# Rows of 64 floats instead of 48 and 50 in the gathered and scattered tables of a four-layer graph network

## The chip, the cores and the metric

The kernel runs on one core of one Trainium2 chip. The metric is the device time of one execution in microseconds (us). Three runs of the kernel before took 16726.7, 16704.65 and 16701.4 us, a median of 16704.65 us.

## The reference, cut to what matters

There are 12500 nodes with 48 features and 400000 edges, sorted by destination. Four layers follow each other, each adding to `x` what it sums over the edges, with a layer norm after each:

```python
x = _layernorm(x + _L0_gnn_ref(x, edge_index, edge_attr_32, ...))      # MLP of (x[dst], x[src], edge), summed by dst
x = _layernorm(x + _L1_gnn_ref(x, src, dst, W, b))                     # x[src] * ci[src], summed by dst
x = _layernorm(x + _L2_gnn_ref(x, edge_index, W, b))                   # norm * x[dst], summed by src
x = _layernorm(x + _L3_gnn_ref(x, edge_index, edge_attr_40, ...))      # gate * x[dst] * cutoff, summed by src
```

The first two layers sum by destination, in which the edges are sorted. The last two sum by source, in which they are not.

## The kernel before, in words

The edges are cut into 125 groups of 25 tiles of 128 edges, and a group into 5 chunks of 5 tiles. A pass over all groups belongs to each layer (pass 0 to pass 3), and behind each pass stands an epilogue (e0 to e3) that works on the nodes in 10 runs of at most 10 blocks of 128 nodes. Each engine runs its own loop over the groups; semaphores alone order them, and between stages all engines meet at a barrier.

Pass 0 and pass 1 gather the source node's row for each edge with indirect DMAs that GpSimd (POOL) issues, one for each tile of 128 edges (lines 489 and 1027). The table of pass 0, `btab`, has rows of 160 floats (640 bytes). The table of pass 1, `y1`, has rows of 48 floats (192 bytes); e0 writes it. TensorE sums a chunk's rows by destination with one-hot matmuls (line 1208), and then the chunk's buffer is free for the next group.

Pass 1 also works out a place for each edge, ordered by source (`uidx`), stores the gates of layer 3 for later, and fills the DRAM tensor `order` with zeros, one store of `zero` on the ScalarE queue in each group (line 1004). `order` has a row for each edge and for padding. A row was OW = 50 floats (200 bytes): 48 features, one more for layer 3's weight, and the low 7 bits of the source (column MW = 49).

Pass 2 and pass 3 are one function, `scatter_pass`. In each group TensorE looks up destination rows (line 1630), ScalarE and VectorE form the messages in `msg`, and POOL scatters each tile of 128 message rows to `order` (line 1487), again one indirect DMA for each tile, 3125 in a pass. There is one `msg` buffer for each chunk, so ScalarE waits at the start of a chunk until the scatter of the same chunk of the group before has landed (`sc[c]`). From group 40 on, blocks of `order` are read back while later groups are scattered: SyncE loads them in four buffers `ordb` (line 1434), VectorE makes a one-hot matrix from the low bits (line 1516), TensorE multiplies (line 1616), and VectorE adds the sums to `agg` (line 1528). The groups come in six parts (40, 28, 20, 15, 12, 10). At the first group of each later part SyncE waits until everything of the parts before has landed; after the last group, 9 more blocks are read, with no scatter beside them. The SyncE loop also loads the ids, windows and edge data of each group, in the same queue as the loads of `order`.

Of the kernel before, what the change touches and what calls it, by code (L numbers as in the profile page):

```python
# [6 lines left out]
F32, BF16, I32, I16 = mybir.dt.float32, mybir.dt.bfloat16, mybir.dt.int32, mybir.dt.int16  # L7
# [12 lines left out]
P = 128  # L20
CT = 5
NCH = 5
GT = CT * NCH
# [3 lines left out]
F = 48  # L27
# [11 lines left out]
GROUPS = (40, 28, 20, 15, 12, 10)  # L39
PARTS = len(GROUPS)  # L40
OW = MW + 1
RB = (10, 10, 10, 10)
LINE = 16
RT = sum(RB)
# [44 lines left out]
def gnn(nc, a, out):  # L89

    pl = Plan(*a["size"])
    N, E, NT, NG, NB, NP = pl.N, pl.E, pl.NT, pl.NG, pl.NB, pl.NP

    def dram(name, shape, dt=F32):
        return nc.dram_tensor(name, shape, dt, kind="Internal").ap()

    d = dict(
        ids16=dram("ids16", [1, E], I16),
        meta=dram("meta", [NG, NCH + 1], I32),
        atab=dram("atab", [NP, H0]),  # L100
        btab=dram("btab", [NP, BW]),
        esrc=dram("esrc", [P, NT, G]),
        degs=dram("degs", [NB, P]),
        y1=dram("y1", [NP, F]),
        y2=dram("y2", [NP, YW]),
        htab=dram("htab", [NP, MW]),
        gates=dram("gates", [P, NT, F]),
        hist=dram("hist", [P, PARTS, CT * NB]),
        order=dram("order", [P * pl.TT, OW]),
        blocks=dram("blocks", [pl.NS, RT], I32),  # L110
    )
    ctx = ExitStack()
    with ctx:
        def sb(name, shape, dt=F32):
            return ctx.enter_context(nc.sbuf_tensor(name, shape, dt))

        r = dict(
            x=sb("x", [P, NB, F]),
            iota_row=sb("iota_row", [P, P]),
            iota_row_bf=sb("iota_row_bf", [P, P], BF16),  # L120
            iota_p=sb("iota_p", [P, 1]),
            ident=sb("ident", [P, P]),

            meta=sb("meta_row", [1, NG, NCH + 3], I32),
            basef=sb("basef", [P, NG + 1, NCH]),
            outdeg=sb("outdeg", [P, NB]),
            indeg=sb("indeg", [P, NB]),
            ci=sb("ci", [P, NB]),
            dis=sb("dis", [P, NB]),
            mult=sb("mult", [P, NB]),  # L130
            acc=sb("acc", [P, NP]),
            regs={}, kept={},
        )
        r["agg"] = r["acc"]
        assert 2 * NB * MW <= NP
        ps = ctx.enter_context(nc.psum_tensor("ps", [P, 8 * BANK], F32))
        with nc.sbuf_tensor("degrow", [1, NP], F32) as degrow:
            r["degrow"] = degrow
            prologue(nc, pl, a, d, r, ps)
            pass0(nc, pl, a, d, r, ps)  # L140
            epilogue0(nc, pl, a, d, r, ps)
        r["uidx"] = sb("uidx", [P, NT], I32)
        r["lof"] = sb("lof", [P, NT], BF16)
        r["cw"] = sb("cw", [P, NT])
        r["adapt"] = sb("adapt", [P, NT])
        pass1(nc, pl, a, d, r, ps)
        epilogue1(nc, pl, a, d, r, ps)
        pass2(nc, pl, a, d, r, ps)
        epilogue2(nc, pl, a, d, r, ps)
        pass3(nc, pl, a, d, r, ps)  # L150
        epilogue3(nc, pl, a, d, r, ps, out)
# [545 lines left out]
def per_block(column, count):  # L697

    return bc(column.rearrange("p (b o) -> p b o", o=1), [P, count, F])


def epilogue0(nc, pl, a, d, r, ps):
# [5 lines left out]
    with Stage(nc, "e0") as s:  # L708
# [2 lines left out]
        degt = s.sb("degt", [NB, P])  # L711
        bias = s.sb("bias", [P, 2, RUN, F])
        sq = s.sb("sq", [P, 2, RUN, F])
        y = s.sb("y", [P, NB, F])
        total = s.sb("total", [P, NB])
        squares = s.sb("squares", [P, NB])
        std = s.sb("std", [P, NB])
# [4 lines left out]
        eps = s.sb("eps", [P, 1])  # L722
        um = [ps[:, k * BANK:k * BANK + RUN * F].rearrange("p (b f) -> p b f", f=F) for k in range(2)]
        degp = ps[:, 4 * BANK:4 * BANK + NB]
        w_in, deg_out, deg_in, degp_ready, indeg_set = (s.sem(k) for k in ("w_in", "deg_out", "deg_in", "degp_ready", "indeg_set"))
        eps_set, deg_ready, root_ready, ci_ready = (s.sem(k) for k in ("eps_set", "deg_ready", "root_ready", "ci_ready"))
        mm, self_bias, biased, taken, summed, centred = (s.sem(k) for k in ("mm", "self_bias", "biased", "taken", "summed", "centred"))
        sq_ready, var_ready, std_ready, self_v, normed, y_ready, y_out = (s.sem(k) for k in (
# [3 lines left out]
        @block.sync  # L732
        def _(sp):
            sp.dma_start(d["degs"].rearrange("(o b) p -> o (b p)", o=1), r["degrow"][:, :]).then_inc(deg_out, 16)
            sp.dma_start(w2[:, :], a["W2_0"]).then_inc(w_in, 16)
            sp.dma_start(b2[:, :], a["b2_0"].rearrange("(o h) -> o h", o=1).to_broadcast([P, F])).then_inc(w_in, 16)
            sp.wait_ge(deg_out, 16)
            sp.dma_start(degt[:, :], d["degs"]).then_inc(deg_in, 16)
            for c, (b, k) in enumerate(runs):
                sp.wait_ge(y_ready, c + 1)  # L740
                sp.dma_start(d["y1"][b * P:(b + k) * P, :].rearrange("(b p) f -> p b f", p=P), y[:, b:b + k, :]).then_inc(y_out, 16)
            sp.wait_ge(y_out, n * 16)
# [15 lines left out]
        @block.gpsimd  # L758
        def _(pool):
            g = nc.gpsimd  # L760
            pool.wait_ge(w_in, 32)
            pool.wait_ge(indeg_set, 1)

            def add_bias(c):
                b, k = runs[c]
                g.tensor_tensor(bias[:, c % 2, 0:k, :], bc(b2[:, None, :], [P, k, F]), per_block(r["indeg"][:, b:b + k], k), ALU.mult).then_inc(self_bias, 1)
                pool.wait_ge(self_bias, c + 1)
                g.tensor_tensor(x[:, b:b + k, :], x[:, b:b + k, :], bias[:, c % 2, 0:k, :], ALU.add).then_inc(biased, 1)

            def scale_rows(c):  # L770
                b, k = runs[c]
                pool.wait_ge(normed, c + 1)
                g.tensor_tensor(y[:, b:b + k, :], x[:, b:b + k, :], per_block(r["ci"][:, b:b + k], k), ALU.mult).then_inc(y_ready, 1)

            for c in range(n):
                add_bias(c)
            pool.wait_ge(ci_ready, 3)
            for c in range(n):
                scale_rows(c)
# [18 lines left out]
        @block.vector  # L798
        def _(dve):
            v = nc.vector  # L800
            v.memset(eps[:, :], LN_EPS).then_inc(eps_set, 1)
            v.tensor_scalar(deg1[:, :], r["outdeg"][:, :], 1.0, None, ALU.max).then_inc(deg_ready, 1)
            v.tensor_scalar(some[:, :], r["outdeg"][:, :], 0.0, None, ALU.is_gt).then_inc(ci_ready, 1)
# [40 lines left out]
def pass1(nc, pl, a, d, r, ps):  # L844
# [19 lines left out]
    segments = [(lo, hi, [q for q in range(PARTS) if pl.begin[q] <= lo][-1]) for lo, hi in zip(cuts, cuts[1:])]  # L864
    with Stage(nc, "l1") as s:
        sd = s.sb("sd", [P, GT, 2], I32)
        rows = s.sb("rows", [P, GT, F])
        ohe = s.sb("ohe", [P, GT, WN])
        drel = s.sb("drel", [P, GT])
        dcolf = s.sb("dcolf", [P, GT])  # L870
# [2 lines left out]
        hot = s.sb("hot", [P, NCH, CT, NB], BF16)  # L873
        prod = s.sb("prod", [P, NCH, CT, NB])
        rank = s.sb("rank", [P, GT])
        ranki = s.sb("ranki", [P, GT], I32)
        place = s.sb("place", [P, 2, GT], I32)
        placef = s.sb("placef", [P, 2, GT])
        rowf = s.sb("rowf", [P, GT])
# [10 lines left out]
        begun = s.sb("begun", [MOST, PARTS, NB])  # L890
        block_no = s.sb("block_no", [MOST, PARTS, RT])
        blk = s.sb("blk", [MOST, PARTS, RT], I32)
        zero = s.sb("zero", [P, pl.ZT * OW])
        eat = s.sb("eat", [2 * EB, 2 * NCH * HE])
        w1 = s.sb("w1", [2 * EB, 2 * F])
        w2 = s.sb("w2", [2 * F + 1, 2 * F])
# [66 lines left out]
        @block.scalar  # L963
        def _(act):
            order = d["order"].rearrange("(p t) f -> p (t f)", t=TT)
            KZ = pl.ZT * OW
            act.dma_start(hist[:, :, :], d["hist"]).then_inc(hist_in, 16)
            act.sem_inc(gate_copied, 2)
            act.sem_inc(gate_out, 32)
# [61 lines left out]
        def _(dve):  # L1031
# [39 lines left out]
            def group(g, part, turning):  # L1071
# [36 lines left out]
                dve.wait_ge(cum_read, (g + 1) * NCH + 1)  # L1108
                ranks = links(dve, self_rank, g * 7)
                ranks(v.tensor_reduce(rank[:, :], prod[:, :, :, :].rearrange("p c t b -> p (c t) b"), AX, ALU.add))  # L1110
                ranks(v.tensor_copy(ranki[:, :], rank[:, :]))
                ranks(v.tensor_scalar(place[:, 0, :], ranki[:, :], P - 1, None, ALU.bitwise_and))
                ranks(v.tensor_scalar(place[:, 1, :], ranki[:, :], P.bit_length() - 1, None, ALU.arith_shift_right))
                ranks(v.tensor_copy(placef[:, :, :], place[:, :, :]))
                ranks(v.scalar_tensor_tensor(rowf[:, :], placef[:, 0, :], float(TT), placef[:, 1, :], ALU.mult, ALU.add))
                v.tensor_scalar(r["uidx"][:, ds(g * GT, GT)], rowf[:, :], float(pl.step0[part] * RT), None, ALU.add).then_inc(self_rank, 1)
# [33 lines left out]
        def _(pe):  # L1150
# [13 lines left out]
            def group(g, turning):  # L1164
# [35 lines left out]
                with pe.Fori(0, rounds) as k:  # L1200
                    w = before + k
                    n = w * NCH
                    pe.wait_ge(acc_added, n + 1)
                    pe.wait_ge(ohe_ready, w + g + 1)
                    for c in range(NCH):
                        pe.wait_ge(gat[c], (g + 1) * 16 * CT)
                        for j in range(CT):
                            last = t.matmul(hacc[:, c, :], rows[:, c * CT + j, :], ohe[:, c * CT + j, :],  # L1208
                                            start=(j == 0), stop=(j == CT - 1))
                        last.then_inc(row_free, 1)  # L1210
                    pe.wait_ge(row_free, n + NCH + 5)
                    pe.sem_inc(acc_ready, 1)
# [146 lines left out]
def scatter_pass(nc, pl, a, d, r, ps, layer):  # L1359
# [20 lines left out]
    LAST = len(RB) - 1  # L1380
    with Stage(nc, f"l{layer}") as s:
        dstb = s.sb("dstb", [WN, 2 * GE], I16)
        msg = s.sb("msg", [P, GT, OW])
        win = s.sb("win", [WN, 2 * SET])
        oht = s.sb("oht", [WN, GE])
        nid = ps[0:WN, 7 * BANK + P:7 * BANK + P + NCH]
        uring = s.sb("uring", [P, GT], I32)
        zero = s.sb("zero", [P, 1])
        ordb = [s.sb(f"ordb{b}", [P, RB[b], OW]) for b in range(len(RB))]
        assert len(set(RB)) == 1 and RB[0] <= LINE  # L1390
        blk = s.sb("blk", [1, 2, len(RB), LINE], I32)
        ohs = [s.sb(f"ohs{b}", [P, RB[b], P]) for b in range(len(RB))]
# [100 lines left out]
        def _(dve):  # L1493
# [5 lines left out]
            v.memset(zero[:, :], 0.0)  # L1499
            if gated:  # L1500
                v.memset(gate[:, :, :], 1.0)
            else:
                dve.sem_inc(logit_made, 1)
                v.memset(msg[:, :, :], 0.0)
# [545 lines left out]
```

## Time and profile before

| what | value |
|---|---|
| median of three runs | 16704.65 us |
| the three runs | 16726.7, 16704.65, 16701.4 us |
| span of the profiled execution | 16721.1 us |
| its mean granted TensorE clock | 0.629 |
| PE busy | 12086.6 us (72%) |
| POOL busy | 12152.9 us (73%) |
| DVE busy | 9036.3 us (54%) |
| ACT busy | 3218.9 us (19%) |
| DMA, mean | 79 GB/s |

The profiled execution's own time is given only as its span, from the first to the last instruction. It is 16.5 us above the median and lies between the fastest and the slowest of the three runs. Busy times are those of one profiled execution. An engine that is busy for most of the span need not set the end; the idle time in front of its instructions, and what ended it, tells more. POOL's busy time in an indirect DMA is the time of the instruction on POOL and not that of the data on the DMA engines.

### The profile page before, as it was taken

What the parts mean: (1) busy time and instruction counts of PE and PEld (TensorE: products, weight loads), DVE (VectorE), ACT (ScalarE), POOL (GpSimd) and SP (SyncE); (2) the same over time, 40 slices, a digit from 0 to 9 for tenths busy, and PEclk for the clock granted to TensorE, in tenths of its full rate; (3) what the DMA queues carried; (4) which work ended last, traced back from release to release, by engine and by line L of the source; (5) the groups of instructions that cost most, each with busy time, mean ns of one, the idle gap of its engine ahead of it and who ended that gap; (6) DMA issues with size and microseconds to landing.
All of it is one profiled execution on the core that took longest, in us unless ns stands there. A gap on an engine that the chain in (4) does not pass through costs nothing. (4 is left out here: it accounts for less than half of the span.)

```text
span 16721.1 us, 272828 instructions
## 1 busy us (share of the span) xinstructions
PE 12086.6 (72%) x57442; PEld 11023.7 (66%) x57443; DVE 9036.3 (54%) x22074; ACT 3218.9 (19%) x9623; POOL 12152.9 (73%) x12612
## 2 busy tenths in 40 slices
PE   7888878887666666666533488988863339888886
PEld 6777777777444444444433488888863338888886
DVE  4776766776554444444422366666652126666667
ACT  1111111111211111111111111111113333333331
POOL 4777777777777777777677777777737777777773
PEclk9999999999555555555555555555555555555555
DMA  5444444444333333333211122222221112232221
GB/s 131 101 102 101 102 101 102 101 102 90 91 85 83 87 85 83 87 85 84 64 41 41 52 74 72 74 73 73 73 52 47 47 51 81 74 83 78 78 79 51
DMA packets 1447655, 1320.81 MB, mean 79 GB/s; under 512 B 958662, under 2 KB 1304425, under 8 KB 1443052
## 3 DMA queue, kind: packets, MB, share of 16 engines
q0 software_dynamic: 450320, 493.60, 12.7%
q1 hardware_dynamic: 502094, 520.02, 12.7%
q10 hardware_dynamic: 495148, 306.20, 6.4%
q8 instruction: 27, 0.44, 0.0%
q14 instruction: 66, 0.54, 0.0%
HBM read 903.35 MB, written 415.31 MB: 79 GB/s over the span
## 5 line engine op out<-in xcount | busy, mean ns | idle before, releaser
L1487 POOL DMA_INDIRECT order<-l_msg,l_uring x6250 | 6066.5, 971 | 1918.4 <-issue 1843.4
L1630 PE MATMUL ps<-l_win,l_oht 32*128 x12500 | 2729.8, 413 | 1996.1 <-DMA l_win<-htab 833.9
L1630 PEld LDWEIGHTS ps<-l_win,l_oht 32*128 32x128 f32 x12500 | 2684.0, 327 | 2037.5 <-issue 2037.5
L489 POOL DMA_INDIRECT l_rows<-btab,l_sd x3125 | 2978.1, 953 | 1128.5 <-issue 1099.7
L1027 POOL DMA_INDIRECT l_rows<-y,l_sd x3125 | 2958.1, 947 | 971.7 <-issue 924.7
L1616 PE MATMUL ps<-l_ordb,l_ohs 128*128 128x49 f32 x15040 | 3278.8, 414 | 377.3 <-DVE l_ohs L1516 184.8
L1616 PEld LDWEIGHTS ps<-l_ordb,l_ohs 128*128 128x128 f32 x15040 | 3231.1, 332 | 429.5 <-issue 334.2
L1528 DVE TENSOR_TENSOR acc<-acc,ps 128x49 f32 x7520 | 1524.5, 206 | 1319.2 <-issue 702.1
L630 PE MATMUL ps<-l_rhs,l_lhs 64*128 x6250 | 1422.0, 423 | 652.3 <-DVE l_rows L566 458.5
L630 PEld LDWEIGHTS ps<-l_rhs,l_lhs 64*128 64x128 f32 x6250 | 1350.8, 328 | 713.4 <-issue 713.4
L645 PEld LDWEIGHTS ps<-l_ohe,l_hid 128*128 128x128 f32 x6250 | 1343.0, 332 | 34.8 <-issue 34.1
L645 PE MATMUL ps<-l_ohe,l_hid 128*128 128x32 f32 x6250 | 1359.9, 401 | 0.6 <-ACT l_hid L675 0.6
L1655 ACT ACTIVATE l_gate<-l_gin,l_cwa,l_cwg 128x48 f32 x3125 | 1006.6, 412 | 1295.0 <-DVE l_cwa L1538 1272.2
L1516 DVE TENSOR_TENSOR l_ohs<-ps,l_ordb 128x1280 f32<-128x1280 f32 x752 | 1112.5, 1480 | 75.1 <-DMA l_ordb<-order 69.5
L675 ACT ACTIVATE l_hid<-l_rows 128x640 f32<-128x640 f32 x625 | 460.4, 737 | 3496.2 <-DVE l_rows L566 3496.2
L1178 PEld LDWEIGHTS ps<-l_w,l_sil 97*128 97x128 f32 x3750 | 928.0, 327 | 253.2 <-issue 214.3
L1170 PE MATMUL ps<-l_eat,l_w 80*96 x1250 | 899.4, 842 | 254.6 <-issue 254.6
L1546 DVE TENSOR_TENSOR l_oht<-ps,l_dstb 32x640 f32<-32x640 f32 x1250 | 934.2, 804 | 111.0 <-DVE ps L1534 53.6
L1208 PE MATMUL ps<-l_ohe,l_rows 128*48 128x32 f32 x6250 | 547.5, 267 | 611.4 <-DMA l_rows<-y,l_sd 611.2
L1102 DVE TENSOR_TENSOR l_prod<-ps,l_hot 128x490 f32<-128x490 f32 x625 | 416.4, 666 | 1052.3 <-PE ps L1183 1052.3
L1208 PEld LDWEIGHTS ps<-l_ohe,l_rows 128*48 128x48 f32 x6250 | 513.4, 192 | 686.7 <-DMA l_rows<-y,l_sd 628.6
L566 DVE TENSOR_TENSOR l_rows<-l_rows,ps 128x640 f32<-128x640 f32 x625 | 506.0, 810 | 747.7 <-DMA l_rows<-btab,l_sd 561.8
(248 smaller groups left out, 10693.5 us busy)
## 6 DMA issues: line engine op xcount, KB each, us to landing
l_ordb<-order SPq DMA_DIRECT2D x752, 250.0 KB
order<-l_msg,l_uring POOLq DMA_INDIRECT x6250
order<-l_zero ACTq DMA_DIRECT2D x125, 775.0 KB, 4.6
l_dstb<-ids SPq DMA_DIRECT2D x376, 200.0 KB
l_eat<-in_ea40P SPq DMA_DIRECT2D x125, 600.0 KB
gates<-l_gate ACTq DMA_DIRECT2D x125, 600.0 KB
l_gin<-gates SPq DMA_DIRECT2D x125, 600.0 KB
l_rows<-btab,l_sd POOLq DMA_INDIRECT x3125
```

The source lines that it names most:

```text
L489: pool.indirect_dma_start(rows[:, t, :], None, d["btab"], bass.IndirectOffsetOnAxis(ap=sd[:, t, 0:1], axis=0)).then_inc(gat[c], 16)
L630: last = t.matmul(pre[c % 2][:, j * P:(j + 1) * P], lhs[:, c * CE + j * P:c * CE + (j + 1) * P], window, start=True, stop=True)
L645: last = t.matmul(hacc[:, c, :], hid[:, c * CT + j, :], ohe[:, c * CT + j, :], start=(j == 0), stop=(j == CT - 1))
L1027: pool.indirect_dma_start(rows[:, t, :], None, d["y1"], bass.IndirectOffsetOnAxis(ap=sd[:, t, 0:1], axis=0)).then_inc(gat[c], 16)
L1208: last = t.matmul(hacc[:, c, :], rows[:, c * CT + j, :], ohe[:, c * CT + j, :], start=(j == 0), stop=(j == CT - 1))
L1487: pool.indirect_dma_start(d["order"], bass.IndirectOffsetOnAxis(ap=uring[:, t:t + 1], axis=0), msg[:, t, :], None).then_inc(sc[c], 16)
L1516: v.tensor_tensor(ohs[b][:, :, :], bc(count_row[:, None, :], [P, RB[b], P]), bc(lo, [P, RB[b], P]), ALU.is_equal).then_inc(ohs_ready, 1)
L1528: v.tensor_tensor(cols, cols, red[b % 2][:, k * MW:(k + 1) * MW], ALU.add).then_inc(agg_added, 1)
L1546: v.tensor_tensor(oht[:, chunk_edges(c)], bc(nid[:, c:c + 1], [WN, CE]), dstb[:, ds((g % 2) * GE + c * CE, CE)], ALU.is_equal).then_inc(oh ...
L1616: done = t.matmul(red[b % 2][:, k * MW:(k + 1) * MW], ohs[b][:, k, :], ordb[b][:, k, 0:MW], start=True, stop=True)
L1630: done = t.matmul(look[c][:, j, :], oht[:, c * CE + j * P:c * CE + (j + 1) * P], win[:, ds((w % 2) * SET + c * LW, LW)], start=False, stop ...
L1655: done = nc.scalar.activation(gate[:, t, 0:F], gin[:, ds(g % 2, 1), t, :].rearrange("p o f -> p (o f)"), ACT.Identity, bias=cwa[:, t:t + 1 ...
```

## The change

The pitch of `order` and of `y1` in DRAM becomes 64 floats (256 bytes), and so does that of the buffers that are copied to or from them: `y` in e0, `rows` and `zero` in pass 1, `msg` and `ordb` in passes 2 and 3. A scatter moves 256 bytes a row instead of 200, a gather of pass 1 256 instead of 192, a load of `ordb` 2560 contiguous bytes a partition instead of 2000. The computed columns stay the same. The padding is set to zero once on VectorE: in e0 (with a semaphore that SyncE waits on before the first store of `y1`), in pass 2 as part of the whole `msg` and in pass 3 by one more instruction. `ranki` is dropped and its values go through `place[:, 1, :]`.

```diff
+PITCH = 64
-        y1=dram("y1", [NP, F]),
+        y1=dram("y1", [NP, PITCH]),
-        order=dram("order", [P * pl.TT, OW]),
+        order=dram("order", [P * pl.TT, PITCH]),
...
-        y = s.sb("y", [P, NB, F])
+        y = s.sb("y", [P, NB, PITCH])
...
+            sp.wait_ge(pads_set, 1)
             for c, (b, k) in enumerate(runs):
                 sp.wait_ge(y_ready, c + 1)
...
-                g.tensor_tensor(y[:, b:b + k, :], x[:, b:b + k, :], ...
+                g.tensor_tensor(y[:, b:b + k, 0:F], x[:, b:b + k, :], ...
...
+            v.memset(y[:, :, F:PITCH], 0.0).then_inc(pads_set, 1)
             v.memset(eps[:, :], LN_EPS).then_inc(eps_set, 1)
...
-        rows = s.sb("rows", [P, GT, F])
+        rows = s.sb("rows", [P, GT, PITCH])
-        ranki = s.sb("ranki", [P, GT], I32)
-        zero = s.sb("zero", [P, pl.ZT * OW])
+        zero = s.sb("zero", [P, pl.ZT * PITCH])
-            KZ = pl.ZT * OW
+            KZ = pl.ZT * PITCH
...
-                ranks(v.tensor_copy(ranki[:, :], rank[:, :]))
-                ranks(v.tensor_scalar(place[:, 0, :], ranki[:, :], P - 1, None, ALU.bitwise_and))
-                ranks(v.tensor_scalar(place[:, 1, :], ranki[:, :], P.bit_length() - 1, None, ALU.arith_shift_right))
+                ranks(v.tensor_copy(place[:, 1, :], rank[:, :]))
+                ranks(v.tensor_scalar(place[:, 0, :], place[:, 1, :], P - 1, None, ALU.bitwise_and))
+                ranks(v.tensor_scalar(place[:, 1, :], place[:, 1, :], P.bit_length() - 1, None, ALU.arith_shift_right))
...
-                            last = t.matmul(hacc[:, c, :], rows[:, c * CT + j, :], ohe[:, c * CT + j, :],
+                            last = t.matmul(hacc[:, c, :], rows[:, c * CT + j, 0:F], ohe[:, c * CT + j, :],
...
-        msg = s.sb("msg", [P, GT, OW])
+        msg = s.sb("msg", [P, GT, PITCH])
-        ordb = [s.sb(f"ordb{b}", [P, RB[b], OW]) for b in range(len(RB))]
+        ordb = [s.sb(f"ordb{b}", [P, RB[b], PITCH]) for b in range(len(RB))]
...
             if gated:
                 v.memset(gate[:, :, :], 1.0)
+                v.memset(msg[:, :, OW:PITCH], 0.0)
```

## Rows read from the trace of the kernel before

**Rows 1.** Stages by window: pass 1, pass 2 in two stretches, its end with e2.
```profile
core 0: us, PE busy (x) PEld busy (x) DVE busy (x) ACT busy (x) POOL busy (x), PEclk, DMA share, GB/s
4227.00:8146.00 3919.00, 2667.57 (x12658) 1873.05 (x12658) 1840.55 (x4164) 652.91 (x1294) 2950.11 (x3117) 0.51 0.34 85
8232.00:9508.00 1276.00, 440.49 (x2015) 432.10 (x2014) 268.68 (x518) 195.84 (x800) 970.92 (x1001) 0.50 0.15 41
9508.00:12219.00 2711.00, 2403.06 (x11002) 2362.79 (x11001) 1704.43 (x4832) 429.41 (x1680) 2054.25 (x2117) 0.50 0.27 73
12219.00:12474.00 255.00, 201.54 (x922) 195.92 (x922) 185.27 (x508) 31.64 (x90) 38.76 (x35) 0.50 0.22 52
```

**Rows 2.** Costliest groups: busy us, mean ns of one, idle before, releasers.
```profile
L1487 POOL DMA_INDIRECT order<-l_msg,l_uring x6250 | 6066.5, 971 | 1918.4 <-issue 1843.4 <-ACT l_uring L1666 55.2 <-DVE l_msg L1555 19.2
...
L489 POOL DMA_INDIRECT l_rows<-btab,l_sd x3125 | 2978.1, 953 | 1128.5 <-issue 1099.7 <-ACT l_hid L675 21.1 <-DMA l_sd<-in_sd 7.8
L1027 POOL DMA_INDIRECT l_rows<-y,l_sd x3125 | 2958.1, 947 | 971.7 <-issue 924.7 <-PE ps L1208 25.9 <-DMA l_sd<-in_sd 21.1
```

**Rows 3.** The same lines alone: duration ns min/median/max.
```profile
L1487 POOL DMA_INDIRECT order<-l_msg,l_uring x6250: 964/972/1066, 8221.8 to 16455.0; - x196
...
L1027 POOL DMA_INDIRECT l_rows<-y,l_sd x3125: 939/947/3126, 4216.6 to 8133.9; - x196
...
L489 POOL DMA_INDIRECT l_rows<-btab,l_sd x3125: 942/949/1415, 191.2 to 4128.0; - x196
```

**Rows 4.** DMA queues, pass 2 with reading (9508 to 12219): packets, MB, share.
```profile
q1 hardware_dynamic: 85643, 142.77, 20.5%
q0 software_dynamic: 67747, 54.33, 6.8%
```

**Rows 5.** Timeline, early pass 3: a scatter and the wait for its landing.
```profile
12475.08 0.97 POOL L1487 DMA_INDIRECT order<-l_msg,l_uring  x1 [0.30 <-issue]
...
12477.36 0.21 ACT L1665 ACTIVATE l_msg<-lof 128x5 f32 x1 [1.22 <-DMA order<-l_msg,l_uring]
```

**Rows 6.** Waits of VectorE over the whole span: total us, times, longest.
```profile
DVE l_ohs L1516 <- DMA l_ordb<-order: 69.5, 12, 23.6
```

**Rows 7.** Waits of POOL in pass 3 (12474 to 16467).
```profile
POOL order L1487 <- issue: 905.4, 2968, 0.3
POOL order L1487 <- ACT l_uring L1666: 32.0, 85, 1.7
POOL order L1487 <- DVE l_msg L1555: 19.2, 63, 0.3
```

**Rows 8.** DMA issues: KB each, us from issue to landing where known.
```profile
l_ordb<-order SPq DMA_DIRECT2D x752, 250.0 KB
...
order<-l_zero ACTq DMA_DIRECT2D x125, 775.0 KB, 4.6
...
y<-e_y SPq DMA_DIRECT2D x2, 192.0 KB
```

**Rows 9.** Timeline, tail of pass 3, one block to the next.
```profile
16505.39 1.48 DVE L1516 TENSOR_TENSOR l_ohs<-ps,l_ordb 128x1280 f32<-128x1280 f32 x1
...
16522.93 1.48 DVE L1516 TENSOR_TENSOR l_ohs<-ps,l_ordb 128x1280 f32<-128x1280 f32 x1
```

**Rows 10.** Timeline at the starts of pass 1, pass 2 and e0.
```profile
4210.56 1.35 DVE L1045 MEMSET l_zero<- 128x1550 f32 x1 [0.27 <-issue]
...
8207.12 1.10 DVE L1504 MEMSET l_msg<- 128x1250 f32 x1 [0.33 <-issue]
...
8213.50 8.12 POOL L1479 MEMSET acc<- 128x9604 f32 x1
...
8221.80 1.06 POOL L1487 DMA_INDIRECT order<-l_msg,l_uring  x1 [0.18 <-issue]
...
4160.49 0.26 DVE L809 COPY indeg<-ps 128x98 f32<-128x98 f32 x1 [6.26 <-PE ps L756]
```

**Rows 11.** Timeline at the start of pass 3: what POOL waits for.
```profile
12463.49 1.07 POOL L1487 DMA_INDIRECT order<-l_msg,l_uring  x1 [6.45 <-ACT l_uring L1666]
```

More of the change, by code:

```diff
@@ L724, in epilogue0 @@
         degp = ps[:, 4 * BANK:4 * BANK + NB]
-        w_in, deg_out, deg_in, degp_ready, indeg_set = (s.sem(k) for k in ("w_in", "deg_out", "deg_in", "degp_ready", "indeg_set"))
+        w_in, deg_out, deg_in, degp_ready, indeg_set, pads_set = (s.sem(k) for k in ("w_in", "deg_out", "deg_in", "degp_ready", "indeg_set", "pads_set"))
         eps_set, deg_ready, root_ready, ci_ready = (s.sem(k) for k in ("eps_set", "deg_ready", "root_ready", "ci_ready"))
@@ L772, in scale_rows @@
                 pool.wait_ge(normed, c + 1)
-                g.tensor_tensor(y[:, b:b + k, :], x[:, b:b + k, :], per_block(r["ci"][:, b:b + k], k), ALU.mult).then_inc(y_ready, 1)
+                g.tensor_tensor(y[:, b:b + k, 0:F], x[:, b:b + k, :], per_block(r["ci"][:, b:b + k], k), ALU.mult).then_inc(y_ready, 1)
             for c in range(n):
```

## The prediction

> **What bounds the kernel now.** I read four views, in this order. The first is the windows by stage, to see which engine is full where. In pass 2 POOL runs 1001 scatters in 1276 us before the blocks are read back, and 2117 in 2711 us while they are, 1.27 and 1.28 us each, though PE goes from 35% to 89% busy and the DMA share from 0.15 to 0.27 [rows 1]. So something keeps one pace through both halves, and it is not PE, VectorE or the DMA engines.
>
> The second is the list of costliest groups. The three lines of indirect DMAs have 6066.5 + 2978.1 + 2958.1 us busy and 1918.4 + 1128.5 + 971.7 us idle before them: 16021 us of a span of 16721. Of the 4019 us idle, 3868 are "issue" and only 150 are waits for another engine or a DMA [rows 2]. The reader is to see that POOL issues one indirect DMA after another, each for about 0.97 us with some 0.3 us of its own between two, and that the kernel is as long as 12500 of these plus the prologue, the epilogues and the two tails. PE's 72% is beside it.
>
> The third is the same three lines alone, with minimum, median and maximum. A scatter takes 964 at least and 972 in the median, a gather of pass 1 939 and 947, a gather of pass 0 942 and 949 [rows 3]. The two gathers differ in row size by a factor of 3.3 (640 against 192 bytes) and by 2 ns in the median. The fourth is the timeline where a buffer is reused, at the starts of stages, and in a tail; these come below.
>
> **The change, part by part.** *The scatters and gathers themselves, on the path.* 6250 scatters go from 200 to 256 bytes a row and 3125 gathers from 192 to 256. The number of instructions and of rows is the same. No row of the trace has 256-byte rows, so I bound the price by the nearest ones. By the two gathers it is 2 ns for 448 bytes in the median, 6 ns in the mean (953 against 947) [rows 2, 3]. Scaled to 64 and 56 bytes a row, the mean gives (6 / 448) x (64 x 3125 + 56 x 6250) = 7.4 us in all, the median 2.5 us. Below nothing: the scatter is 24 ns slower than the gather with nearly the same row [rows 2], and the trace doesn't say whether this comes with scattering or with a row of 200 bytes; if all of it went, it would be 6250 x 24 ns = 150 us less. I take 0. The scatter's mean is also 970 ns in both halves of pass 2 (970.92 / 1001 and 2054.25 / 2117) though the DMA share nearly doubles [rows 1], so the instruction's time doesn't follow what the DMA engines do.
>
> The Trainium skill (DMA: Bandwidth & Descriptors, How a descriptor splits into AXI transactions) says that a transfer is cut at 256-byte boundaries, the first piece being read from the boundary below its start. By that rule rows of 200 bytes at a pitch of 200 need a second piece at 24 of the 32 possible offsets, and rows of 256 at a pitch of 256 never do, so the DMA engines would have less to do for more bytes. In the sum this is worth nothing, since the indirect DMAs' packets take 6.8% of the engines' time [rows 4]; it would count only if POOL's instruction were paced by them, which is the first rival. No row tells a cut row from a whole one.
>
> *Landing.* A scatter of 32 KB lands later than one of 25 KB. Whoever waits for it is ScalarE, which rewrites that chunk's `msg`. In pass 3 the last scatter of a chunk ends on POOL at 12476.05 us and ScalarE goes on at 12477.36, 1.3 us later [rows 5]. POOL comes back to this chunk after 20 more scatters, 20 x 1.28 = 25.5 us. Less 1.3 us and about 1 us for the copies and VectorE's product, 23 us are free. Price 0; it would take a landing 18 times as long.
>
> *Loads of `order`.* 752 loads grow from 250 to 320 KB. The nearest row with a time is the zero store, 775 KB in 4.6 us, 168 KB/us [rows 8], so 70 KB are at most 0.42 us. VectorE waited for such a load 12 times of 752 [rows 6]: at 10 first groups of a part and at 2 tails. The 740 others are hidden, in the tail too: there one block follows the next after 17.5 us (16505.39 to 16522.93) [rows 9], set by PE's 40 matmuls and VectorE's sums, with each buffer loaded as soon as PE has left it. The 2 tails pay 0.42 us each, 0.8 us. At the first groups POOL would have to run dry to pay. In pass 3 its waits beyond issue are 51 us over 148 times, none over 1.7 us [rows 7]; I let the 5 first groups of pass 3 pay in full, 2.1 us, and those of pass 2 nothing. Behind such a load SyncE has the next group's ids, windows and gates queued; their delay is the same 0.42 us, not one more.
>
> *Zero stores.* 125 stores on ScalarE's queue go from 775 to 992 KB, 4.6 to 5.9 us at the same rate, once in 31 us beside DMA engines at a share of 0.34 [rows 1, 8]. Only the end of pass 1 waits for them. Price 0; cover gone, 1.3 us.
>
> *`y1` in e0.* The last store, 192 KB, becomes 256 KB, and the stage's end waits for it: 64 / 168 = 0.4 us. The new memset of 98 x 16 elements: the memsets of 1250 and 1550 elements take 1.10 and 1.35 us, 0.83 ns an element [rows 10], so 1.3 us. It stands in front of VectorE's preparation, which then idles 6.26 us for a transpose of PE before line 809 [rows 10]: hidden; without that cover, 1.3 us. SyncE's new wait is met before e0's first normed run exists. Behind it stand only those stores.
>
> *The other memsets.* `zero` grows by 434 elements (0.36 us): VectorE waits on PE afterwards, and POOL's gathers don't need it, 0. `msg` in pass 2 grows by 350 elements, 0.3 us, and this is on the path: the flag behind it lets POOL start, whose 8.12 us memset ends right at the first scatter [rows 10]. The same 0.3 us in pass 3 are covered, since POOL idles 6.45 us before its first scatter for ScalarE, which was held by the load of the gates [rows 11]. `ranki`: the same seven steps, 0. The matmuls and VectorE's compare read the same columns with another step, 0.
>
> Sum: 0 + 0.8 + 2.1 + 0.4 + 0.3 = 3.6 us. The profiled span of 16721.1 becomes 16724.7. The profiled execution stands 16.5 us above the median of the runs, so the same 3.6 us on 16704.65 give 16708.
>
> **The rivals.** *Faster, the scatter's surplus goes.* The 24 ns by which a scatter exceeds a gather come from its row of 200 bytes, and a whole row of 256 costs what a gather does. For it: the surplus is in the minimum too (964 against 939) [rows 3]. Against it: 24 ns over 128 rows is 0.2 ns a row, more like a fixed step of scattering, and the gathers of 192 and 640 bytes show no such effect. It gives 16708 - 150 = 16558 us, and decides from 6 ns, a quarter of it.
>
> *Slower, POOL's instruction grows with the bytes.* Place: lines 1487 and 1027. If the whole step of 6 ns between the means of the two gathers came with the first 64 bytes, it would be 9375 x 6 ns = 56 us, 16764 us. It decides from 3.2 ns for each of the 9375, (33.4 - 3.6) / 9375. For it: the sign of the difference is right. Against it: the median difference is 2 ns for 448 bytes, and the means of pass 0 carry waits of its own, its maximum is 1415 [rows 3].
> The Trainium skill (DMA: Bandwidth & Descriptors, Anatomy of one DMA) fits a DMA of POOL's by 2.0 us plus the bytes over 436 GB/s; as an estimate by that page, 7168 and 8192 bytes more would be 16 and 19 ns, 162 us in all and 16870 us if POOL paid them. The trace speaks against it: by that fit the gathers of pass 0 would take 131 ns more than those of pass 1.
>
> *Slower, the reading half falls behind.* SyncE's loads of 1.25 times the bytes delay the edge data. The two queues' shares are 20.5% and 6.8% [rows 4]; times 1.28 they make 35%. It would need POOL to wait 0.35 us more in each of the 85 reading groups of one pass to reach 30 us (16738 us). Nothing points there.
>
> **How the numbers follow.** The forecast has 0.88, the faster rival 0.06, the two slower ones 0.04 and 0.01, and 0.01 on top for a slower cause that I don't see. 0.2% is 33 us, about what a measurement of this kernel can tell from no change. So faster 0.06, same 0.88, slower 0.06. For the range I take 2 ns either way for each of the 9375 indirect DMAs, the difference of the gathers' medians, 18.8 us, and half the spread of the three runs, 12.7 us: 16708 less and plus 31.5 is 16677 to 16740. It leaves out the rivals, 0.12 or a little less.
>
> **What the profile after would show.** Right: lines 1487 and 1027 at 972 and 947 ns in the median within 2 ns, POOL's waits as now, the scatter's bytes up by 28% with the same packets, 12 waits of line 1516 for a load, a tail block of 17.5 us. Wrong: a median of line 1487 near 948 (faster), or of either line up by 4 ns and more (slower); a wait of POOL for `l_uring` of more than 1 us in ordinary groups; line 1516 waiting in the tail for each block.

## The result and the profile after

| | before | after |
|---|---|---|
| median of 8 runs | 16703.87 us | 16753.04 us |
| lowest to highest | 16701.4 to 16726.7 | 16743.08 to 16759.15 |
| span of the profiled execution | 16721.1 us | 16748.8 us |

The change makes the kernel slower by 49.2 us, a ratio of 1.0027 (95% interval 1.0017 to 1.0037). The forecast was 16708 us with a range of 16677 to 16740, and it is outside.

First the costliest groups after, the three lines of indirect DMAs as in [rows 2] (busy us, mean ns of one, idle before, releasers).

```profile
L1489 POOL DMA_INDIRECT order<-l_msg,l_uring x6250 | 6053.7, 969 | 1919.5 <-issue 1840.8 <-ACT l_uring L1669 61.3 <-DVE l_msg L1558 17.4
...
L490 POOL DMA_INDIRECT l_rows<-btab,l_sd x3125 | 2976.2, 952 | 1128.1 <-issue 1100.7 <-ACT l_hid L676 16.4 <-DMA l_sd<-in_sd 10.9
...
L1029 POOL DMA_INDIRECT l_rows<-y,l_sd x3125 | 2957.1, 946 | 1011.8 <-issue 926.4 <-DMA l_sd<-in_sd 74.5 <-PE ps L1210 11.0
```

The instructions themselves got no dearer: 969 and 946 ns after 971 and 947. What grew is the idle time in front of the gathers of pass 1, from 971.7 to 1011.8 us, and inside it one releaser: the load of the ids, `l_sd`, from 21.1 us [rows 2] to 74.5. The scatters of passes 2 and 3, with 1.75 times as many added bytes in all as the gathers (6250 x 56 against 3125 x 64 for each partition), idle as long as before.

The same lines alone, as in [rows 3] (duration ns min/median/max, first to last start).

```profile
L1489 POOL DMA_INDIRECT order<-l_msg,l_uring x6250: 963/969/1063, 8259.0 to 16482.6; - x196
...
L1029 POOL DMA_INDIRECT l_rows<-y,l_sd x3125: 938/944/3180, 4213.9 to 8170.7; - x196
...
L490 POOL DMA_INDIRECT l_rows<-btab,l_sd x3125: 941/946/1432, 190.8 to 4125.6; - x196
```

Pass 1, from its first to its last gather, takes 3956.8 us, where it took 3917.3 [rows 3]: 39.5 us more. The scatters, from the first of pass 2 to the last of pass 3, take 8223.6 us after 8233.2: 9.6 us less. All three lines are faster by 3 ns in the median, the gathers of pass 0 too, which nobody touched. Experiment 1 shows that this pace changes between executions of one program, so it is no effect of the change. At equal pace pass 1 has lost about 3 ns x 3125 = 9 us more than the 39.5, some 48 us, which is nearly the whole result.

Now one boundary between two groups in pass 1, before and after (timeline; start us, us, engine). Before:

```profile
5842.52 3.41 PE L1208 MATMUL ps<-l_ohe,l_rows 128*48 128x32 f32 x40
...
5843.54 0.34 ACTq L1004 DMA_DIRECT2D order<-l_zero  x1
5843.75 8.44 SPq L943 DMA_DIRECT2D l_sd<-in_sd  x5
...
5849.41 0.95 POOL L1027 DMA_INDIRECT l_rows<-y,l_sd  x1 [0.35 <-issue]
```

After:

```profile
5861.70 3.41 PE L1210 MATMUL ps<-l_ohe,l_rows 128*48 128x32 f32 x40
...
5862.72 0.34 ACTq L1006 DMA_DIRECT2D order<-l_zero  x1
5862.93 3.62 SPq L945 DMA_DIRECT2D l_sd<-in_sd  x4
...
5867.19 0.94 POOL L1029 DMA_INDIRECT l_rows<-y,l_sd  x1 [0.30 <-issue]
5869.25 0.94 POOL L1029 DMA_INDIRECT l_rows<-y,l_sd  x1 [1.12 <-DMA l_sd<-in_sd]
```

The reader is to see a chain. PE's matmuls free the chunks' buffers, SyncE at once loads the ids of the next group, while POOL still gathers the last chunk of its group, and POOL's next gather needs them. Before, the gather starts 5.66 us after the issue of the load (5843.75 to 5849.41), with 0.35 us of idle in front of it where 0.30 is usual: the ids came in the last moment. After, it is 6.32 us (5862.93 to 5869.25) and an idle of 1.12 us. And 0.21 us before the load of the ids, ScalarE issues the zero store, in both kernels. So there was hardly any slack to spend, and the larger zero store stands in front of the ids.

### The profile page after: what moved, and what is told of

Same layout as the page of the kernel before. It is cut to its first block and busy times, and to the rows that moved or that the text cites. A ratio compares the mean times of both kernels' runs of the same rounds, so it can differ in the third digit from the quotient of the medians.

```text
span 16748.8 us, 272831 instructions
## 1 busy us (share of the span) xinstructions
PE 12099.1 (72%) x57442; PEld 11028.9 (66%) x57443; DVE 9029.3 (54%) x22076; ACT 3216.9 (19%) x9623; POOL 12137.1 (72%) x12612
## 3 DMA queue, kind: packets, MB, share of 16 engines
q1 hardware_dynamic: 502094, 574.73, 13.5%
## 5 line engine op out<-in xcount | busy, mean ns | idle before, releaser
L1029 POOL DMA_INDIRECT l_rows<-y,l_sd x3125 | 2957.1, 946 | 1011.8 <-issue 926.4
```

Source lines behind the costliest of these rows:

```text
L1029: pool.indirect_dma_start(rows[:, t, :], None, d["y1"], bass.IndirectOffsetOnAxis(ap=sd[:, t, 0:1], axis=0)).then_inc(gat[c], 16)
```

## The experiments

All times are medians of 11 runs (run 12: 8), each against runs of the kernel before that were made together with it on the same chip. There are three such series, each on another chip: runs 1 to 4, with the kernel before at 16700.0 us, runs 5 to 8, with it at 16698.85, and runs 9 to 12, with it at 16728.68.

**1. The kernel before, again.** No edit.

> The kernel before, unchanged, for a second profile. Theory A (pass 1's loads of ids are just in time before the change, and the larger zero store delays them): time 16704 +- 5 us, POOL's waits for l_sd in pass 1 under 25 us and the interval between two gathers of pass 1 1251 ns or less in the median. Theory B (POOL's own pace differs from program to program): the same medians as in the first profile of before, 947 and 972 ns. If instead the medians are 944 and 969 ns, POOL's pace differs from one execution to the next of the same program, by about 2.5 ns x 12500 = 31 us, and the profile of before was taken in a slower one.

16699.04 us (ratio 0.9999, 0.999 to 1.0008). Its profiled execution took 16730.94 us, the other ten 16696.87 to 16703.17, and its POOL lines read as in [rows 2]:

```profile
L1487 POOL DMA_INDIRECT order<-l_msg,l_uring x6250 | 6069.9, 971 | 1919.1 <-issue 1848.4 <-ACT l_uring L1666 50.5 <-DVE l_msg L1555 19.5
...
L1027 POOL DMA_INDIRECT l_rows<-y,l_sd x3125 | 2960.4, 947 | 971.7 <-issue 922.8 <-PE ps L1208 27.7 <-DMA l_sd<-in_sd 21.2
```

One program, one chip, and 32 us between the profiled execution and the rest. The first profile of before has the same longer durations. Its span and that of the profile after are 27.7 us apart, so these two hide some 20 us of the 49.

**2. The pitch in `y1` alone.** From the changed kernel:

```diff
-        order=dram("order", [P * pl.TT, PITCH])
+        order=dram("order", [P * pl.TT, OW])
...
-            KZ = pl.ZT * PITCH
+            KZ = pl.ZT * OW
```

and `zero`, `msg` and `ordb` likewise.

> Only y1, y and rows have the pitch of 64; order, zero, msg and ordb stay at 50 floats. Theory A (the zero store): the zero store is 775 KB as before, so at most 0.1 us a group from later landing gathers, 16704 to 16711 us. Theory C (the wider gathers take the DMA engines' time from the ids): most of the 49 us stay, 16730 us or more, with POOL waiting over 45 us for l_sd.

16706.46 us, ratio 1.0003 (0.9994 to 1.0012): 6.5 us, and the interval holds no change. POOL waits 23.3 us for the ids, 6 times; the waits of about 0.8 us in every second group are not there. Small ones are: in front of the first gather of 83 groups POOL idles 0.4 to 0.7 us instead of 0.30, put down to "issue", which has grown from 924.7 to 950.7 us.

```profile
L1029 POOL DMA_INDIRECT l_rows<-y,l_sd x3125 | 2952.2, 945 | 986.8 <-issue 950.7 <-DMA l_sd<-in_sd 23.3 <-PE ps L1210 12.8
```

**3. The pitch in `order` alone.** The other half: `y1`, `y` and `rows` back to F.

> Only order, zero, msg and ordb have the pitch of 64; y1, y and rows stay at 48 floats. Theory A: the zero store is 992 KB, so 16740 to 16750 us, POOL waiting for l_sd in pass 1 about 60 us, every second group. Theory C: 16706 us, with the waits of before.

16731.51 us, ratio 1.0018 (1.0009 to 1.0027), 31.5 us, below the 16740 expected at least. The halves sum to 38 us, both together cost 49.

```profile
L1027 POOL DMA_INDIRECT l_rows<-y,l_sd x3125 | 2960.2, 947 | 995.5 <-issue 927.0 <-DMA l_sd<-in_sd 59.0 <-PE ps L1208 9.5
```

59.0 us of waiting for ids in pass 1, with gathers of the old width. The change to the tensor of passes 2 and 3 costs its time in pass 1.

**4. The changed kernel, zero store moved.**

```diff
                 for c in range(NCH):
                     copy_gates(c)
+                    if c == 0:
+                        act.nop(nofuse=True)
+                        act.dma_start(order[:, ds(g * KZ, KZ)], zero[:, :]).then_inc(z_out, 16)
...
-                act.wait_ge(hot_ready, (g + 1) * NCH)
-                act.nop(nofuse=True)
-                act.dma_start(order[:, ds(g * KZ, KZ)], zero[:, :]).then_inc(z_out, 16)
```

> The changed kernel, with the zero store issued behind the first gate copy of a group instead of at the end, so that it runs when no ids are being loaded. Same bytes in all. Theory A: the waits for l_sd go nearly to zero, 16700 us (16695 to 16708). Theory C: the bytes still compete, 16745 us or more.

16698.33 us, ratio 0.9999 (0.999 to 1.0008). The whole loss is gone, with every pitch and every byte still there. In the DMA issues of pass 1 (5000 to 7500 us; last column from issue to landing) the zero store, which landed in 4.6 us before [rows 8], reads in the changed kernel

```profile
order<-l_zero ACTq DMA_DIRECT2D x79, 992.0 KB, 5.2
```

and here, away from the ids,

```profile
order<-l_zero ACTq DMA_DIRECT2D x80, 992.0 KB, 3.9
```

**5. The zero store cut, 217 KB of it moved.** The 775 KB stay in the old place.

```diff
+                        act.dma_start(order[:, ds(g * KZ, REST)], zero[:, 0:REST]).then_inc(z_out, 16)
...
-                act.dma_start(order[:, ds(g * KZ, KZ)], zero[:, :]).then_inc(z_out, 16)
+                act.dma_start(order[:, ds(g * KZ + REST, KZ - REST)], zero[:, REST:KZ]).then_inc(z_out, 16)
```

> The changed kernel, its zero store cut in two: 775 KB stay where they were, 217 KB go behind the first gate copy. Same bytes in all, same gathers. Theory A (the bytes of the zero store beside the loads of ids set the delay): as with the pitch in y1 alone, 16706 us (16700 to 16713). Theory C (the wide gathers delay the loop whatever the zero store is): over 16725 us.

16709.78 us, ratio 1.0006 (0.9997 to 1.0015). As the theory of the zero store had it. But it can't tell the bytes of the group from the form of the one store in front of the ids.

**6. The kernel before with 217 KB more.**

```diff
                 act.dma_start(order[:, ds(g * KZ, KZ)], zero[:, :]).then_inc(z_out, 16)
+                act.dma_start(d["spare"][:, ds(g * 434, 434)], zero[:, 0:434]).then_inc(z_out, 16)
```

> The kernel before, with a second store of 217 KB of zeros to an unused tensor right behind the zero store of each group. No pitch is changed. Theory A: the extra bytes alone do what the pitch of order did, 16725 to 16740 us, POOL waiting for l_sd in every second group of pass 1. Rival (the pitch of 256 bytes does it, by addresses or by the reads of order, not by bytes): 16700 us.

16695.56 us, ratio 0.9998 (0.9989 to 1.0007). No loss at all. My theory in its first form, that extra bytes beside the ids delay them, fails here: the same bytes in the same place, in a DMA of their own, cost nothing. But the other theory that this run was to speak for, the pitch as such, has been refuted by run 4. What is left is the form of the store. In the packet records of the traces (5000 to 7500 us of pass 1), each zero store is 128 packets of data, one a partition, or 8 for each of the 16 DMA engines if they share them evenly, and the larger pitch makes the packets longer, not more. The last column is the mean, over 117 groups, of the time from the issue of chunk 0's ids to the end of their last packet.

```
kernel               bytes of a zero packet    ns of one   us, ids of chunk 0
before               6200                      261         3.92
changed              7936                      328         4.50
2 y1 alone           6200                      262         3.97
3 order alone        7936                      319         4.41
4 moved              7936 (elsewhere)          323         2.25
6 217 KB more        6200, then 1736           259, 73     3.98
```

The ids of a chunk are 128 packets too, of 40 bytes and 11 ns each. In the two boundaries shown above, not one of them starts before the zero store has started its last packet (us from the issue of the ids):

```
kernel    zero packets, first and last start    packets of chunk 0's ids, first and last start
before    1.65 to 3.60                          3.82 to 3.94
changed   1.60 to 4.10                          4.40 to 4.52
```

So it is in 77 of 115 groups of the kernel before and in 48 of the changed one. In most of the others the two take turns: in one of them 16, 32, 32, 31 and 17 zero packets and, 0.5 us behind, 17, 32, 31 and 39 packets of ids start in successive half microseconds. Either way the ids are through about 0.3 us after the last zero packet starts (3.63 and 3.93 in the mean, 4.15 and 4.50 after the change), having let 8 zero packets pass on each engine: 8 x (328 - 261) ns = 0.54 us, against 0.58 measured. In 89 of the 115 groups of run 6 the ids of chunk 0 begin behind the last packet of the old store and in front of the first of the extra one. The Trainium skill (DMA: Bandwidth & Descriptors, Queues, rings and completion order) says that a DMA engine goes round the queues that have work and changes only between packets, where its packet is a batch of typically 9 to 17 descriptors. If such a batch is what one DMA has on an engine, here 8 records of data and one of 4 bytes, the trace agrees in the 77 groups, and in those with turns it doesn't.

**7. The kernel before with 434 KB more**, twice the extra store of run 6.

> As the run before, with 434 KB extra instead of 217 KB. Theory A with every second group paying the delay: the ids of chunk 0 land another 0.5 us later, 62 pairs of groups, so 30 us more again, 16755 to 16775 us. If the delay saturates, since the ids' packets wait only for the packet in front of them, about the same time as with 217 KB.

16716.3 us, ratio 1.0011 (1.0002 to 1.002), 17.5 us. Neither the doubling nor nothing. The ids of chunk 0 take 3.95 us, as without it. What grows is another stretch of the same loop, from POOL's last gather of a group to the issue of chunk 4's ids: 3.07 us after 2.74. The last extra packet ends 5.20 us after the issue of the ids (4.59 in run 6), while the group's last gather runs from 4.28 to 5.22 us, so bytes behind the ids cost too, from some size on.

**8. The kernel before, zero store moved.** The edit of run 4.

> The kernel before, with its 775 KB zero store moved behind the first gate copy. Theory A: little is left to gain, since before POOL hardly waited: 16690 to 16700 us. If it is 20 us faster or more, the kernel before was already losing time to the zero store.

16692.2 us, ratio 0.9996 (0.9987 to 1.0005). The median is 6.7 us lower, the interval holds no change. The kernel before stood at the edge, hardly over it.

**9. The changed kernel, zero store halved in place.**

```diff
-                act.dma_start(order[:, ds(g * KZ, KZ)], zero[:, :]).then_inc(z_out, 16)
+                act.dma_start(order[:, ds(g * KZ, KZ // 2)], zero[:, 0:KZ // 2]).then_inc(z_out, 16)
+                act.dma_start(order[:, ds(g * KZ + KZ // 2, KZ - KZ // 2)], zero[:, KZ // 2:KZ]).then_inc(z_out, 16)
```

> The changed kernel, its zero store of 992 KB in the same place, but as two DMAs of 496 KB one behind the other. Theory P (the packets of the ids take turns with those of the zero store, so what counts is how long one zero packet is: 328 ns after the change, 262 before): the 8 packets of the first ids on each engine pass beside 8 packets of about 165 ns, the ids of chunk 0 land over 1 us earlier than in the changed kernel, 16695 to 16705 us. Theory A in its first form (the bytes beside the ids): 16745 us or more.

16730.92 us against 16728.68 for the kernel before in this series, ratio 1.0001 (0.9992 to 1.001), with the changed kernel at 16774.84 beside it (run 12). In absolute numbers the expectation missed, since the kernel before too took some 29 us more than in the first two series; this holds for runs 10 to 12 as well. In the comparison it is right: 44 us come back through one more DMA. A zero packet now has 3968 bytes and takes 164 ns, and the ids of chunk 0 take 3.33 us, where 4.50 - 8 x 0.164 = 3.19 was to be expected. But the run can't speak for packets against DMAs: each half is again 128 packets, half as long, so the DMA in front of the ids has half the bytes as well.

```profile
5867.87 0.34 ACTq L1006 DMA_DIRECT2D order<-l_zero  x1
5868.08 3.69 SPq L945 DMA_DIRECT2D l_sd<-in_sd  x4
5868.37 0.82 ACTq L1007 DMA_DIRECT2D order<-l_zero  x1
...
5873.68 0.94 POOL L1030 DMA_INDIRECT l_rows<-y,l_sd  x1 [0.30 <-issue]
```

In this timeline the second half is issued 0.29 us after the ids. By the packet records the 128 packets of chunk 0's ids start from 3.11 to 3.31 us after their issue, behind the first half's last packet (2.99) and in front of all of the second half's; so it is in 81 of 115 groups. POOL's gathers follow each other with 0.30 us between them all through the boundary.

**10. The changed kernel, 775 KB and then 217 KB in place.** As run 9 with the cut at `pl.ZT * OW`.

> The changed kernel, its zero store in the same place as 775 KB and, right behind it, 217 KB. Theory P: the first ids pass beside packets of the old size, so as with the pitch in y1 alone, 16700 to 16712 us. Theory A in its first form: 16745 us or more.

16730.96 us, ratio 1.0001 (0.9992 to 1.001). All 992 KB are in the old place and at most 2.3 us are lost, within the uncertainty: the one DMA in front of the ids decides, not the bytes of the group.

**11. The kernel before, zero store halved in place.**

> The kernel before, its zero store of 775 KB as two DMAs of 388 KB in the same place. Theory P: the ids land earlier, but little was waited for, so as with the zero store moved, 16690 to 16698 us. If before had free time of its own there, 16699 us as before.

16726.08 us, ratio 0.9999 (0.999 to 1.0008). The ids take 3.04 us instead of 3.92, and it gains 2.6 us, within the uncertainty.

**12. The changed kernel, again.**

> The changed kernel, unchanged, beside these: 16745 to 16755 us, and in its profile every second group of pass 1 with a wait of 0.8 us for the ids.

16774.84 us, ratio 1.0028 (1.0018 to 1.0039), 46 us over the kernel before in the same series, 20 us above the range expected. Only 36 groups have an idle over 0.7 us this time, and 38 more one of 0.4 to 0.7. The profiled execution has POOL's longer durations this time:

```profile
L1489 POOL DMA_INDIRECT order<-l_msg,l_uring x6250 | 6069.8, 971 | 1920.8 <-issue 1842.5 <-ACT l_uring L1669 56.3 <-DVE l_msg L1558 22.0
L490 POOL DMA_INDIRECT l_rows<-btab,l_sd x3125 | 2979.0, 953 | 1128.5 <-issue 1099.9 <-ACT l_hid L676 21.1 <-DMA l_sd<-in_sd 7.6
L1029 POOL DMA_INDIRECT l_rows<-y,l_sd x3125 | 2966.9, 949 | 1003.1 <-issue 939.9 <-DMA l_sd<-in_sd 56.2 <-PE ps L1210 7.0
```

971 and 953 ns, the means of the kernel before [rows 2]. In the median it is 972 ns for the scatter and 947 for the gather of pass 1, as before the change [rows 3]: the 25 ns between them have nothing to do with the row of 200 bytes. And the waits for the ids are there at either pace, 56.2 us here.

No version beat the kernel before by more than the uncertainty; the lowest ratio is run 8's.

All runs beside each other, from the semaphore and instruction records of pass 1. "Landed" is the mean time from the issue of chunk 0's ids to the last update of their semaphore, over the 87 to 115 groups in which all 16 updates are recorded. "Surplus" is POOL's idle time in front of the first gather of a group beyond the usual 0.30 us, summed from the third group on.

| kernel | DMA in front of the ids, KB | landed, us | surplus, us | median over before, us |
|---|---|---|---|---|
| before | 775 | 4.77 | 3.3 | |
| changed | 992 | 5.33 | 42.9 | 49.2 |
| 1 before again | 775 | 4.75 | 2.1 | -1.0 |
| 2 `y1` alone | 775 | 4.83 | 13.5 | 6.5 |
| 3 `order` alone | 992 | 5.20 | 27.9 | 31.5 |
| 4 moved | none | 2.87 | 0.6 | -1.7 |
| 5 217 KB moved | 775 | 4.81 | 10.6 | 10.9 |
| 6 217 KB more | 775 | 4.59 | 0.9 | -3.3 |
| 7 434 KB more | 775 | 4.54 | 14.6 | 17.5 |
| 8 before, moved | none | 2.85 | 0.6 | -6.7 |
| 9 halves | 496 | 3.97 | 0.6 | 2.2 |
| 10 775 and 217 KB | 775 | 4.61 | 2.1 | 2.3 |
| 11 before, halves | 388 | 3.68 | 0.6 | -2.6 |
| 12 changed again | 992 | 5.35 | 36.7 | 46.2 |

In no run does the gather start sooner than 0.82 us after the landing, and in the kernel before the median group has just these 0.82 us. Run 7 is the one that loses time by another way.

## Why the prediction was wrong, point by point

**What bounds the kernel: right, but read too far.** POOL sets the pace. From "only 150 us are waits" it was concluded that everything else has room. The 25.9 and 21.1 us in front of line 1027 [rows 2] are 85 and 16 waits. 11.6 us of them belong to the first gather of the pass and 5.3 to the second group. The other 99 are about 0.30 us each, the idle that POOL has anyway: they cost nothing and tell that the release came in the last moment. They were the edge of a loop. From the traces, the loop runs from POOL's last gather of a group over the matmuls of chunk 4 and the issue of its ids (2.75 us), their packets (1.36), VectorE's start (2.50), the work of VectorE and PE up to the matmuls of the rows (17.94), the issue of the next ids (1.22) and their packets (3.92) to POOL's first gather two groups on (1.95), 31.64 us in the mean. POOL alone needs 25 x 1.251 + 0.30 = 31.58 us for the same stretch. After the change the packets take 4.50 us and the first term 2.85, and the mean is 32.27. A delay of this loop costs once in two groups, and the trace after has it so: an idle of 0.96 to 1.17 us, in place of 0.30, in nearly every second group up to group 98, few of this size later.

**The scatters and gathers: right.** Priced at 0, within 2 ns. Medians of 972 and 947 ns became 969 and 944, and 971 and 949 in the mean in run 12, the durations that the kernel before also has [rows 2]. The faster rival (the surplus of scattering goes) is refuted. The slower rival (POOL's instruction grows with the bytes) ends on the right side for the wrong reason, and that its 16764 us lie near the measured 16753 is luck; its 3.2 ns an instruction are not there, and it would have shown in the scatters, which run as before. The estimate by the Trainium skill (DMA: Bandwidth & Descriptors, Anatomy of one DMA), 162 us if POOL paid for the bytes, is refuted with it. And that the DMA engines would have less to do for more bytes isn't borne out: a scatter's packet of 8 rows takes 104 ns after 78 (pass 2 with reading), 0.051 ns a byte after 0.049, and a gather's 167 ns after 150.

**Landing of the scatters, loads of `order`: right.** These lines of the profile after are the waits of VectorE and POOL, as in [rows 6] and the second row of [rows 7], the latter over both passes:

```profile
DVE l_ohs L1519 <- DMA l_ordb<-order: 73.7, 12, 23.8
```
```profile
POOL order L1489 <- ACT l_uring L1669: 61.3, 154, 6.1
```

12 waits again, 4.2 us longer in sum, where 12 x 0.42 us = 5.0 was the bound. POOL waits 61.3 us after 55.2 [rows 2]. In the tail a block still takes 17.53 us, as in [rows 9] (line 1519 starts at 16528.73 and at 16546.26).

**`y1` in e0 and the memsets: right as far as can be seen.** Between the last indirect DMA of one pass and the first of the next, start to start, the traces have 88.6, 87.9 and 256.9 us before and 88.2, 88.3 and 258.6 after, +1.7 us in sum. With 2.5 us more of gaps at the first groups of pass 3's parts (2.1 had been allowed), 4.2 us stand against the forecast's 3.6. The 1.7 us lie between pass 2 and pass 3, where the forecast had 0.4 and run 12 has 0.8.

**The step that failed: "Zero stores ... Only the end of pass 1 waits for them. Price 0".** The store was asked who waits for it, and not who stands beside it on the DMA engines. Its issue lies 0.21 us before that of ids which POOL needs at once. In its place: 47 us. The intervals over 1.3 us between the starts of two gathers of pass 1 exceed the median interval (1.25 us) by 9.0 us in sum before and by 56.4 after. Runs 3, 4, 5, 9 and 10 show it, each by taking the large DMA in front of the ids away or bringing it alone. The wider gathers add a smaller part: without them the large DMA costs 31.5 us, with them 46 to 49. By themselves the medians give 6.5 and 10.9 us (runs 2 and 5), each within its interval, but the traces of both have the small waits of every second group, 10 and 7 us more of surplus than before. In run 10, wide gathers and all, they are gone. That the mean of the first term of the loop grows by 0.10 us with both halves of the change and by 0.02 with `y1` alone fits a contribution of the gathers, but was not isolated.

**The third rival, edge data delayed by larger loads, was the right kind of cause in the wrong pass.** It looked at the 85 reading groups of pass 2 or 3, where nothing happened, and had a chance of 0.01. "Slower" in all had 0.06.

**Open.** Every DMA of zeros here is 128 packets, so no run tells the length of its packets from the bytes of the DMA. That the ids mostly pass behind a whole DMA speaks for the DMA; the same 992 KB in one DMA of more and shorter packets would decide it, and was not tried. The ids' semaphore comes 0.8 to 0.9 us after their last packet where one whole zero store stands in front of them (in the median; before, changed, runs 1, 2, 3, 5 and 12), and 0.55 to 0.63 where it is away or has a further DMA behind it. This is why run 10 has ids landed earlier than run 5, and its cause was not looked for. The store of the gates, 600 KB, is issued 0.56 us in front of the zero store on the same queue; in run 4, with it alone, chunk 0's ids take 2.25 us, and chunk 4's ids, with neither beside them, 1.4. Moving it was not tried. Nor was why the waits get shorter after group 98, nor the first wait of pass 1, in the second group, of 2 to 12 us in all the traces, which differs between executions and may hold part of the few microseconds of runs 2 and 5.

## What to carry to other kernels

Where one engine sets the pace and others serve it just in time, ask of each transfer that grows which small, urgent load is issued within a microsecond of it, and compare its path with the time the pacing engine needs anyway; 0.6 us was enough for 47. Waits on others in front of the pacing engine that are no longer than its usual idle, in a hundred places, are no remainder but the mark of a loop without slack. A bulk store beside urgent loads is better cut into several DMAs, a small one in front of the loads, or issued at a quiet place of the period; either took back the whole loss here, within the uncertainty.

## What the runs showed of the hardware that was not expected

Loads of 5 KB took 3.92 us behind a store of 775 KB in one DMA, 4.50 us behind one of 992 KB, 3.33 us behind one of 496 KB with as much again behind it, and 2.25 us with the store elsewhere, from issue to last packet. Each of these DMAs was 128 packets. In 77 of 115 groups of the kernel before, all packets of the load started behind the last one of the store. A further DMA of 217 KB behind the first did not count.

POOL's pace in an indirect DMA has two values for one and the same program: 944 and 969 ns or 947 and 972 ns in the median (gather of pass 1 and scatter), some 30 us over 12500 of them. The kernel before took 16700.0 us and 16698.85 in two series and 16728.68 in a third; only runs of one series can be compared to a few microseconds. It is not fixed by the chip alone: in the third series the profiled executions of runs 9 and 10 took 16698.73 and 16708.57 us, with 944 ns a gather, beside ten others each of 16726 to 16737.
